# Second and third layer norm of a cross-attention stage: row sums taken from the additions, squares on ScalarE, the second norm's factors in the first matrix and its shift in biases

## What is computed

```python
z = self_attn(x, Wq1, Wk1, Wv1)
x = layer_norm(x + z, ln1_g, ln1_b)
z = cross_attn(x, context, Wq2, Wk2, Wv2)
x = layer_norm(x + z, ln2_g, ln2_b)
z = jax.nn.relu(x @ fc1_w + fc1_b)
z = z @ fc2_w + fc2_b
return layer_norm(x + z, ln3_g, ln3_b)
```

## Time and profile before

| what | value |
|---|---|
| median of the runs | 1901.94 us (3 runs, 1892.37 to 1902.0) |
| the profiled execution's own time | 1903.14 us |
| its span | 1901.4 us |
| stage 1, from the span's start | to about 767 us |
| stage 2 | about 767 to 1174 us |
| stage 3 | the rest |
| granted TensorE clock, mean | 0.959 |

### The profile page before, as it was taken

How to read it: one execution, slowest core, us unless ns; L and a number is a source line. 1 busy time by engine, 2 the same in 40 slices (tenths; PEclk the granted TensorE clock), 3 DMA queues, 4 the chain that set the end, 5 groups by cost and what they waited for, 6 DMA issues and landing times.

```text
span 1901.4 us, 24451 instructions
## 1 busy us (share of the span) xinstructions
PE 1721.2 (91%) x8254; PEld 1420.2 (75%) x8254; DVE 987.6 (52%) x1872; ACT 462.7 (24%) x772; POOL 340.8 (18%) x462
## 2 busy tenths in 40 slices
PE   7798999969899999688777877999999999999999
PEld 5577888858778887577666765787878787878787
DVE  3455544447364443678888898644342434333411
ACT  3221221113121211232222222322222222222222
POOL 0110000002000000156666664101010000000000
PEclk9798999989999999799999988999999999999999
DMA  4310110022011100624334434310101010101000
GB/s 129 106 44 24 44 34 23 28 74 67 1 56 34 34 23 18 201 77 134 119 128 133 134 117 123 99 56 1 45 1 46 1 45 0 46 0 45 0 23 23
DMA packets 64032, 110.98 MB, mean 58 GB/s; under 512 B 9729, under 2 KB 11777, under 8 KB 63771
## 3 DMA queue, kind: packets, MB, share of 16 engines
q1 hardware_dynamic: 58653, 100.92, 16.6%
q10 hardware_dynamic: 5272, 8.63, 1.5%
HBM read 83.08 MB, written 26.45 MB: 58 GB/s over the span
## 4 chain that ended last, share of the span: by engine, by line
PE 74%; DVE 9%; POOL 7%; issue 5%; DMA 3%; ACT 2%; DVEq 0%; SPq 0%; POOLq 0%; ACTq 0%
PE banks L539 70%; PE banks L549 2%; POOL split L1132 2%; POOL small L1107 2%; POOL tile_x L1148 2%; PE banks L663 1%; POOL small L1105 1%; DVE small L1498 1%; DVE split L1718 1%; DVE plain L1515 1%; DVE plain L1745 1%; ACT split_q L870 1%; DMA codes<-in_L_ffn_fc_scales 1%; ACT split L870 1%; DVE split L1237 1%
## 5 line engine op out<-in xcount | busy, mean ns | idle before, releaser
L539 PE MATMUL banks<-split_q,split 128*128 128x512 f32 x2304 | 588.8, 406 | 18.7 <-POOL split L1132 6.5
L539 PE MATMUL banks<-split 128*128 128x512 f32 (+3 forms) x2388 | 556.6, 383 | 40.6 <-DVE split L1237 21.9
L539 PEld LDWEIGHTS banks<-split_q,split 128*128 128x128 f32 x2304 | 444.6, 196 | 115.5 <-issue 9.8
L539 PEld LDWEIGHTS banks<-split 128*128 128x128 f32 (+1 forms) x2388 | 427.9, 187 | 135.4 <-DVE split L1237 25.9
L539 PE MATMUL banks<-split,split_q 128*128 128x512 f32 (+3 forms) x2208 | 433.5, 351 | 5.4 <-DVE split_q L1237 3.0
L539 PEld LDWEIGHTS banks<-split,split_q 128*128 128x128 f32 x2208 | 357.1, 195 | 53.4 <-issue 5.7
L1105 POOL TENSOR_TENSOR small<-small 128x1 f32<-128x1 f32 (+1 forms) x168 | 56.6, 337 | 1423.5 <-DVE small L1286 708.9
L870 ACT ACTIVATE split<-banks 128x512 fp32r<-128x512 f32 (+5 forms) x234 | 128.7, 560 | 535.5 <-PE banks L663 230.3
L1237 DVE TENSOR_TENSOR split<-banks,split 128x512 fp32r<-128x512 f32 (+5 forms) x234 | 149.4, 640 | 197.1 <-ACT split L870 195.4
L1718 DVE TENSOR_TENSOR split<-plain,split 128x512 fp32r<-128x512 f32 x128 | 89.3, 697 | 227.4 <-ACT split L1077 227.4
L1237 DVE TENSOR_TENSOR split_q<-banks,split_q 128x512 fp32r<-128x512 f32 x68 | 46.9, 690 | 232.9 <-ACT split_q L870 232.9
(11 more groups left out here) (116 smaller groups left out, 999.1 us busy)
## 6 DMA issues: line engine op xcount, KB each, us to landing
plain<-in_x SPq DMA_DIRECT2D x56, 256.0 KB, 2.7
x_scratch<-plain SPq DMA_DIRECT2D x32, 256.0 KB, 2.1
plain<-x_scratch SPq DMA_DIRECT2D x32, 256.0 KB, 4.3
tile_x<-in_x SPq DMA_DIRECT2D x32, 256.0 KB, 5.1
xg_scratch<-tile_x SPq DMA_DIRECT2D x32, 256.0 KB, 2.8
out<-plain SPq DMA_DIRECT2D x32, 256.0 KB, 2.1
tile_x<-x_scratch SPq DMA_DIRECT2D x28, 256.0 KB, 5.9
plain<-xg_scratch SPq DMA_DIRECT2D x7, 1024.0 KB, 5.5
```

The source lines that it names most:

```text
L539: mm = nc.tensor.matmul(out, left(c, l), right(c, r), start=start and c == 0 and (l, r) == PASSES[0], stop=stop and c == chunks - 1 and (l ...
```

## The change

- The row sums. `add_z` and `add_y` write, beside their result, the sum over the 512 features (`accum_out`); `add_y` becomes a `scalar_tensor_tensor` for that. A new [128,1] step (`mean_z`, `mean_y`) makes minus the mean of it.
- The squares. ACT computes the sum of (x - mean) squared with one activation of 128x512 (`square`), which writes the squares as bf16 to a place nobody reads. POOL's two steps work on that sum with 512 times epsilon, so their result is the root's reciprocal divided by the square root of 512; `ROOT` = sqrt(512) is put into the gains.
- The second norm. On DVE it is one `tensor_scalar` of 128x512 in place of two `scalar_tensor_tensor`. The gain (times ROOT) is multiplied into the first matrix as it is split (fc1, per row), and for the residual POOL multiplies where it added before (`gain_x2`). The shift goes through the first matrix into its bias (16 matmuls of one column at the stage's start, one addition to `b1x`), and together with the second bias it enters each `mlp_out` as one more matmul of 2 rows by 512 columns ahead of the twelve (`y_ones`, `y_rows`).
- The third norm keeps its two `scalar_tensor_tensor`.
- The order in `tile2` on DVE, ACT and POOL is written anew. `add_y(3)` now stands behind `lo_x2(2)`, POOL's `norm_y(2)`, `norm_y(3)` stand ahead of `lo_w` and `lo_hid`.
- At the start SP waits for the 16 matmuls before it loads x1, and two more small vectors are loaded at the program's start; one small DMA (2 KB) puts the low part of `y_rows` in its place, and ACT's and PE's next steps wait for it.

Stage 1 and stage 3 are as before.

```diff
...
-DVE1, DVE2, DVE3 = 134, 19, 27
+DVE1, DVE2, DVE3 = 134, 7, 27
...
             sp.wait_ge(fcw_lo, C)
+            sp.wait_ge(b1_full, 1)
...
-            for n, v in enumerate(("ln2_g", "ln2_b", "ln3_g", "ln3_b", "fc2_b")):
+            for n, v in enumerate(("ln2_b", "fc2_b", "ln3_g", "ln3_b", "ln2_g")):
...
+            sp.wait_ge(y_rows_lo, 1)
+            sp.dma_start(y_rows[1:2].bitcast(F32), y_low[1:2].bitcast(F32)).then_inc(y_rows_in, 16)
             sp.wait_ge(fcw_lo, 2 * C)
...
+                nc.tensor.matmul(PS[:, 4 + k % 2], y_ones, y_rows, start=True, stop=False)
                 product(PS[:, 4 + k % 2], lambda f, h: hid2[:, f, h, k * P:(k + 1) * P],
-                        lambda f, h: fc2[:, f, h, :], C, y_full)
+                        lambda f, h: fc2[:, f, h, :], C, y_full, start=False)
...
+            pe.wait_ge(fcw_in[0], 16)
+            for f in range(C):
+                for c in range(C):
+                    mm = nc.tensor.matmul(PS[:, 4, f:f + 1], fc_stage[0][:, c, f * P:(f + 1) * P],
+                                          b2c[:, c:c + 1], start=c == 0, stop=c == C - 1)
+            mm.then_inc(b1_full, 1)
...
+            act.wait_ge(fcw_in[0], 16)
+            for c in range(C):
+                nc.scalar.activation(fc1[:, c, 0, :], fc_stage[0][:, c], copy,
+                                     scale=g2c[:, c:c + 1]).then_inc(fcw_hi, 1)
...
+            def square(n, x, mean, out):
+
+                act.wait_ge(sq_ready, n - 1)
+                act.wait_ge(mean_ready, n)
+                nc.scalar.activation(squares, x, ACT.Square, bias=mean, accum_out=out).then_inc(sq_ready, 1)
...
-            split_fc(1, fc2)
-            for k in range(BT):
-                hi_x2(0, k)
+            square_z(1, 0, 0)
+            square_z(2, 0, 1)
+            hi_x2(0, 0)
+            hi_x2(0, 1)
+            square_z(3, 0, 2)
+            square_z(4, 0, 3)
+            act.wait_ge(vec2_ready, 2)
+            nc.scalar.activation(y_rows, vec2[0:2, 0], copy).then_inc(y_rows_hi, 1)
+            hi_x2(0, 2)
+            hi_x2(0, 3)
+            act.wait_ge(fcw_in[1], 16)
+            for c in range(C):
+                nc.scalar.activation(fc2[:, c, 0, :], fc_stage[1][:, c], copy).then_inc(fcw_hi, 1)
...
+            act.wait_ge(b1_ready, 1)
+            act.wait_ge(y_rows_in, 16)
             hidden(0)
 
             def tile2(t, u, slot, final, last):
+                n = t * 2 * BT + BT
                 if not last:
                     copy_st(t + 1)
                     probs(t + 1, 1 - slot)
+                    square_y(n + 1, slot, 0)
                     hi_p(t + 1)
+                    square_y(n + 2, slot, 1)
+                    square_z(n + 3, 1 - slot, 0)
+                    square_z(n + 4, 1 - slot, 1)
                     hi_x2(t + 1, 0)
+                    square_z(n + 5, 1 - slot, 2)
                     hi_x2(t + 1, 1)
+                    square_z(n + 6, 1 - slot, 3)
+                    square_y(n + 7, slot, 2)
                     hi_x2(t + 1, 2)
+                    square_y(n + 8, slot, 3)
                     hi_x2(t + 1, 3)
                     hi_w(t * 2, q1, w1_unit(u, slot * 2))
...
+            def rstd2(n, sq, out, t=0):
+
+                pool.wait_ge(sq_ready, t * 2 * BT + n)
+                nc.gpsimd.tensor_tensor(out, sq, eps_sum, ALU.add).then_inc(eps2_added, 1)
+                pool.wait_ge(eps2_added, t * 2 * BT + n)
+                nc.gpsimd.tensor_tensor(out, out, half, ALU.pow).then_inc(rstd2_ready, 1)
...
-                nc.gpsimd.tensor_tensor(N[:, slot, k], N[:, slot, k], vec2[:, 4], ALU.add).then_inc(x2_biased, 1)
+                nc.gpsimd.tensor_tensor(N[:, slot, k], N[:, slot, k], vec2[:, 4], ALU.mult).then_inc(x2_gained, 1)
...
-                norm_z(t, 0)
+                norm_y(BT + 1, t, 0)
+                norm_y(BT + 2, t, 1)
+                norm_z(BT + 3, t, 0)
+                norm_z(BT + 4, t, 1)
                 bias_xo(t, 0)
-                norm_z(t, 1)
+                norm_z(BT + 5, t, 2)
+                norm_z(BT + 6, t, 3)
                 bias_xo(t, 1)
-                norm_z(t, 2)
-                norm_z(t, 3)
-                norm_y(t, 0)
+                norm_y(BT + 7, t, 2)
                 bias_xo(t, 2)
-                norm_y(t, 1)
+                norm_y(BT + 8, t, 3)
                 lo_w(t * 2, w1_unit(u, slot * 2))
                 for f in range(C):
                     lo_hid(t + 1, f)
                     if f == 1:
                         bias_xo(t, 3)
-                norm_y(t, 2)
-                norm_y(t, 3)
                 if final:
                     rstd(first, mvX[:, :, 1], rs_x)
...
+            dve.wait_ge(b1_full, 1)
+            nc.vector.tensor_tensor(b1x, b1x, PS[:, 4, 0:C], ALU.add).then_inc(b1_ready, 1)
...
-                                               op0=ALU.mult, op1=ALU.add).then_inc(z_free, 1)
-
+                                               op0=ALU.mult, op1=ALU.add,
+                                               accum_out=sumZ[:, k:k + 1]).then_inc(z_free, 1)
+
+            def mean_z(t, k):
+                dve.wait_ge(z_free, t * BT + 2 + B * NB + k + 1)
+                nc.vector.tensor_scalar(nmuZ[:, k:k + 1], sumZ[:, k:k + 1], -1.0 / E, None,
+                                        ALU.mult).then_inc(mean_ready, 1)
+
+            def norm_z(n, t, slot, k):
+                dve.wait_ge(rstd2_ready, n)
+                nc.vector.tensor_scalar(N[:, slot, k], N[:, slot, k], nmuZ[:, k:k + 1], rsZ[:, k:k + 1],
+                                        ALU.add, ALU.mult).then_inc(x2_ready, 1)
...
+            nc.vector.tensor_scalar(vec2[:, 4], vec2[:, 4], ROOT, None, ALU.mult).then_inc(vec2_ready, 1)
+            nc.vector.tensor_tensor(vec2[:, 0], vec2[:, 0], vec2[:, 1], ALU.add).then_inc(vec2_ready, 1)
...
-                    dve.wait_ge(x2_biased, t * BT + k + 1)
-                    nc.vector.tensor_tensor(x, PS[:, 4 + k % 2], x, ALU.add).then_inc(y_free, 1)
-
-                def begin(k):
-                    return norm_stats(p2, N[:, slot, k], k)
-
-                def mean(k, at):
-                    norm_mean(p2, at, mvE, k)
-
-                def scale(k, n):
-                    return norm_scale(p2, N[:, slot, k], mvE, k, vec2[:, 2], n)
-
-                def shift(k, at, n):
-
+                    dve.wait_ge(x2_gained, t * BT + k + 1)
+                    nc.vector.scalar_tensor_tensor(out=x, in0=PS[:, 4 + k % 2], scalar=1.0, in1=x, op0=ALU.mult,
+                                                   op1=ALU.add, accum_out=sumE[:, k:k + 1]).then_inc(y_free, 1)
+
+                def mean_y(k):
+                    dve.wait_ge(y_free, t * BT + 4 + k + 1)
+                    nc.vector.tensor_scalar(nmuE[:, k:k + 1], sumE[:, k:k + 1], -1.0 / E, None,
+                                            ALU.mult).then_inc(mean_ready, 1)
...
                     softmax(p2, t + 1, 1 - slot)
                     sum_probs(p2, t + 1, 1 - slot)
                     add_y(0)
+                    mean_y(0)
                     lo_probs(t + 1)
                     add_y(1)
-                    norms_z(p2, t + 1, 1 - slot, n0, 0, lambda _: None)
+                    mean_y(1)
+                    add_z(t + 1, 1 - slot, 0)
+                    mean_z(t + 1, 0)
+                    add_z(t + 1, 1 - slot, 1)
+                    mean_z(t + 1, 1)
+                    g0 = scale(n0 + 1, 0)
+                    norm_z(n0 + 3, t + 1, 1 - slot, 0)
+                    norm_z(n0 + 4, t + 1, 1 - slot, 1)
+                    add_z(t + 1, 1 - slot, 2)
+                    mean_z(t + 1, 2)
                     lo_x2(t + 1, 0)
-                    norms_z(p2, t + 1, 1 - slot, n0, 2, lambda n: add_y(2) if n else lo_x2(t + 1, 1))
+                    add_z(t + 1, 1 - slot, 3)
+                    mean_z(t + 1, 3)
+                    lo_x2(t + 1, 1)
+                    add_y(2)
+                    mean_y(2)
+                    norm_z(n0 + 5, t + 1, 1 - slot, 2)
+                    norm_z(n0 + 6, t + 1, 1 - slot, 3)
+                    lo_x2(t + 1, 2)
                     add_y(3)
-                    lo_x2(t + 1, 2)
-                    dve.wait_ge(y_free, t * BT + 4 + BT)
-                    s0 = begin(0)
+                    mean_y(3)
+                    g1 = scale(n0 + 2, 1)
                     lo_x2(t + 1, 3)
-                    mean(0, s0)
-                    s1 = begin(1)
                     scale_w(0)
-                    mean(1, s1)
-                    g0 = scale(0, ny)
+                    shift(n0 + 1, 0, g0)
                     lx1(0)
-                    shift(0, g0, ny)
-                    s2 = begin(2)
-                    g1 = scale(1, ny + 1)
-                    mean(2, s2)
-                    shift(1, g1, ny + 1)
+                    shift(n0 + 2, 1, g1)
                     lx1(1)
-                    s3 = begin(3)
+                    g2 = scale(n0 + 7, 2)
```

(10 more changed lines are left out.)

195 lines of the change are left out of this document (108 added, 87 removed).

## The result

The changed kernel takes 1903.45 us (median of 20 runs, 1899.82 to 1911.35), the kernel before in the same comparison 1898.36 (20 runs): a ratio of 1.0031, 95% interval 1.0020 to 1.0042. So it is 0.3% slower. The forecast was 1863, its range 1846 to 1885. The profiled execution of the changed kernel has a span of 1903.0 us, against 1901.4 before.

A forecast was written before the change was run, and what follows sets the result against it. It took PE's wait for DVE's late softmax in stage 2, with the slow clock behind it, as the bound. 1903.1 - 33 (six tiles) - 9.2 (last tiles) + 2.5 (start) gave 1863 us, range 1846 to 1885.

The forecast's parts named there:

- DVE's work in a tile: Stage 2 tile: removed and added DVE passes leave 6.3 to 10.1 us less work, 27.7 to 31.5 us.
- Hand-overs between DVE's steps: Stage 2 on DVE: each of eight means waits for the addition ahead; 0.32 us each with its wait, 2.6 a tile.
- The passes of the new norm: Second norm on DVE: four added passes a tile, 0.55 us alone, 1.50 beside POOL's work, 2.2 to 6.0 in all.
- contention: Rival, stage 2 tiles: DVE passes stretched by POOL's work keep DVE the bound, a tile takes 41 us; 1881 us, chance 0.18.
- Is DVE early?: Tile's end: DVE reaches the softmax on time, at most 1 us of it not hidden behind `mlp_out(0)`.
- First part: Tile from `mlp_out(0)` to the start of `mlp_out(3)`: only PE's own work is left, 14.8 us in place of 21.6.
- Second part ... 23.9: Tile from `mlp_out(3)` to the next `mlp_out(0)`: 23.3 us before, 1.2 given back, a little regained, 23.9.
- The x2 give-back: Second part of a tile: `mlp_in` waits for the moved `add_y(3)` and `square_y(3)`; with the row matmul 1.2 us more.
- PE's row matmul: Ahead of each `mlp_out`: one added matmul of 512 columns, 0.25 us each, four a tile, 1.0 us on PE's path.
- The last tiles: From the last `mlp_out(0)` to stage 3's first DVE step: 6.8 and 3 us less, 0.6 given back, 9.2 us less.
- The start: Start of stage 2: one-column matmuls (4.6 us), later loads and a 2 KB transfer add 2.5 us, bounds 0 and 7.
- ACT's queue: Rival: ACT's squares and hand-overs stand on PE's path, holding copies PE needs; 9.8 us a tile added, 1935 us, chance 0.05.

The follow-up runs named there:

- after_copy: The changed kernel with ACT's copy of the cross scores moved ahead of the copy of the second unit of codes: 1882.06 us, ratio 0.9910 to the kernel before.
- copy_x2: copy_s94 with ACT's square of the fourth block and a DVE scaling put behind the x2 steps PE waits for: 1866.17 us, ratio 0.9840 to the kernel before.
- after_nob1: The changed kernel without the sixteen one-column matmuls, the addition to the first bias and the waits for them: 1887.31 us, ratio 0.9936 to the kernel before.
- after_s94: The changed kernel with the head of PE's stage 3 loop set at slot 94 of a 256-instruction block: 1895.54 us, ratio 0.9982 to the kernel before.
- copy_s94: The changed kernel with ACT's copy of the scores moved and PE's stage 3 loop head at slot 94: 1871.75 us, ratio 0.9852 to the kernel before.
- before_s231: The kernel before with the head of PE's stage 3 loop set at slot 231 of a 256-instruction block: 1902.69 us, ratio 1.0015.
- before_pad72: The kernel before with 36 spare matmuls (72 PE instructions) at the start of stage 2: a single run, 1901.2 us.
- before_s239: The kernel before with the head of PE's stage 3 loop set at slot 239 of a 256-instruction block: a single run, 1903.07 us.
- before_pad96: The kernel before with 48 spare matmuls (96 PE instructions) at the start of stage 2: 1907.26 us, ratio 1.0041.
- after_again: The changed kernel run once more, unaltered, for a second profile: 1903.14 us, ratio 1.0022 to the kernel before.

## Why the prediction was wrong, step by step

Between the two profiles the start of stage 2 cost 4.8 us, the six tiles gave 6.9, the last tiles 8.0, and stage 3 took 11.6 back: + 1.5 in all, where + 2.5 - 33 - 9.2 was forecast. The sum also set out from 1903.1, a profiled execution 4.7 us above the median of 20 runs.

- *DVE's work in a tile*, 27.7 to 31.5: right, 28.5. *ACT*, 19 us: right, 18.4, a square with its read 0.91 in place of 0.82.
- *Hand-overs between DVE's steps*: sized too high. An addition, its read and the mean were priced 1.15 us together. After_copy shows 0.90 from one addition to the next, with the mean starting 0.04 us behind the end of the read:

```profile
909.84 0.75 DVE L1574 SCALAR_TENSOR_TENSOR plain<-banks,small,plain 128x512 f32<-128x512 f32 x1
910.51 0.08 DVE L1574 DVE_READ_ACCUMULATOR plain<-banks,small,plain 128x1 f32 x1
910.63 0.15 DVE L1580 TENSOR_SCALAR small<-small 128x1 f32<-128x1 f32 x1
910.74 0.75 DVE L1574 SCALAR_TENSOR_TENSOR plain<-banks,small,plain 128x512 f32<-128x512 f32 x1
```

  I had gone by the idle time ahead of `bn_aggr` and against the Trainium skill (VectorE: DVE Perf Modes, The DRAIN you can't avoid), which lets the semaphore cost nothing; here the trace is on the page's side.
- *The passes of the new norm* took 0.55 and 1.50 in after_copy (913.12 and 914.11), 0.99 on average in the changed kernel: inside the bounds. Beside POOL's work they are stretched, as the contention rival had it, but PE waits for them only 1.5 us over the whole of after_copy (2.8 in the changed kernel).
- *"Is DVE early?"*: right in what it says. `turn_probs` no longer waits.
- *First part*, 14.8: 17.5 in the changed kernel (906.96 to 924.45), with 2.5 of slow clock in it; 15.5 in after_copy, 0.5 of it the row matmuls' extra.
- *"Second part ... 23.9"*: **this step failed**. It counted the steps given back for x2 and took the end of the tile as it was. I never walked ACT's order there: the new order of DVE puts `scale_w(1)` behind a scaling, ACT's `hi_w` waits for it, and `copy_st`, which PE needs, stands behind `hi_w`. From the row matmul of `mlp_out(3)` to the next tile's it took 26.0 us (924.45 to 950.44), and the idle time brought the low clock back for `mlp_out(0)`, 2.5 us in the first part. With the copy moved the same stretch takes 24.0 (916.25 to 940.23), and the tile 39.4 against the forecast's 38.5; with the x2 steps in front as well, 38.7. So six tiles gave 7 us and not 33, from 264.8 to 257.9; in the seven further profiles with the tiles of before they take 260.8 to 265.3, so 7 is the upper end and some 3 the lower.
- *The x2 give-back*, 1.2 us a tile: copy_x2 shows 0.8.
- *PE's row matmul*, 0.25 each: undersized. 0.42, of which 0.7 us a tile are exposed.
- *The last tiles*, - 9.2: - 8.0 (`turn_scores(7)` to stage 3's first step 48.3 before, 40.3 now).
- *The start*, + 2.5 with bounds 0 and + 7: undersized, inside the bounds. The matmuls take 6.83 us where 4.6 were counted, DVE waits for them, and the loads stand behind them; with all that hangs on them they cost 8.2 by after_nob1, and `turn_scores(0)` is 8.6 later. The first tile then gives 3.8 back, so at `turn_scores(1)` + 4.8 is left. The row I priced by, 0.58 for two records, gives 0.29 a record; I took a record for a matmul.
- *Stage 3*: no term in the sum, and none of the rivals had it. That the change adds 97 PE instructions ahead of a loop was not looked at, and costs 8 us (after_s94 against the changed kernel) to 10 (copy_s94 against after_copy).

The rivals: "contention" had the right place (DVE's stretched end of tile) and the wrong wait; "ACT's queue" named the right queue, but searched it only for copies behind squares, and the one that mattered stands behind a copy of codes.

## What to carry to other kernels

When a change cuts one engine's work, walk the order of every engine at the end of the tile as well as where the old wait was: an instruction that PE needs, queued behind one that it doesn't, inherits the latter's wait, and this took 21 us here. And look at where a change shifts code: after a change in the number of PE instructions ahead of a loop, an idle time at the back branch without a releaser is worth a run with the loop's head set elsewhere before the change itself is blamed.

## What the runs showed of the hardware

- PE's loop of 1692 instructions is not fetched again when it starts at slot 94 (49 packets of 16 KB), and is when it starts at slot 159, 231 or 239 (67). The packets come some 28 us apart in steady work and closer at the branch: in the changed kernel at 1431.2, 1435.2 and 1439.4, the first 3.1 us ahead of the end of the product that runs (1434.3).
- Fetching again is free as long as the head's block lasts until the next one has come. Idle time by instructions left there: 0 to 0.36 us with 25 (before_s231; 0.44 and 0.49 in before_pad72, with about as many), 1.16 to 1.32 with 17 (before_s239), 3.08 to 3.14 with some three (before_pad96); 2.93 to 3.56 in the changed kernel, after_again and after_copy. The period grows by 3.4 us where the clock stays at its upper level (before_pad96) and by 4.3 to 6.1 where it falls to the lower one behind the stall (the other three, the next twelve matmuls 4.20 to 5.28 in place of 2.88).
- The Trainium skill (Runtime: NRT & Kernel Launch, Instruction fetch mechanics) says that only two blocks of 16 KiB are held and that a branch out of this window stalls. For PE these traces differ: a loop of 7 blocks is held, and of the branches that do fetch most cost nothing.
- An fp32 matmul of one column with 128 x 128 weights takes 0.43 us, in two records, 0.21 from one to the next; a row matmul of 2 rows by 512 columns 0.42 to the next product's start, more than a full 128 x 512 one in a chain (2.88 for twelve).
